# Graph attention and message passing on one core: relative node numbers spread over the partitions by TensorE in place of a DMA broadcast

## What is computed

```
# layer 0 (heads H = 4 of C = 32), per edge e = (src, dst):
alpha = sum(q[dst] * k[src], -1) / sqrt(C)
a     = softmax of alpha over the edges of one dst
conv  = segment_sum(a * v[src], dst) + x @ Wskip.T + bskip
#   then output projection, layer norm, a 512 wide MLP, layer norm
# layer 1, per edge: w = MLP(radial embedding of edge_weight)
#   messages = products of w, up(x)[src] and the direction edge_attr_3
out = segment_sum(messages, dst) @ W_out
```

## Time and profile before

| | |
|---|---|
| three runs | 2977.77, 2978.21, 2989.45 us, median 2978.21 |
| span of the profiled execution | 2979.6 us (what lies around it is not given apart) |
| busy, share of the span | PE 62%, PE weight loads 48%, DVE 56%, ACT 43%, POOL 53% |
| mean granted TensorE clock | 0.729 of full speed |
| DMA | 271.84 MB, mean 91 GB/s |

### The profile page before, as it was taken

One profiled execution on the slowest core, in us unless ns is written; L12 is line 12 of the kernel. 1 busy time (PEld: TensorE's weight loads), 2 busy tenths in 40 slices (PEclk: granted clock), 3 DMA queues, 4 the chain that ended last, 5 costly groups with the idle time before them and its releaser, 6 DMA issues. The chain is left out here.

```text
span 2979.6 us, 37370 instructions
## 1 busy us (share of the span) xinstructions
PE 1851.9 (62%) x9706; PEld 1441.9 (48%) x9706; DVE 1673.9 (56%) x4970; ACT 1271.8 (43%) x3058; POOL 1569.1 (53%) x1617
## 2 busy tenths in 40 slices
PE   3255454454554554454568177778787887887787
PEld 2244344354443444444555055555555555555556
DVE  2355555555554555554666055666656655666668
ACT  0245444455454555454545033434334334334345
POOL 4345455555555555555302756666666666666640
PEclk7556666656666666666678577888888778888889
DMA  6456454545555555544301211111111111111110
GB/s 213 135 140 170 134 136 133 138 135 144 142 137 137 140 143 138 145 130 134 109 2 35 53 39 43 45 47 44 45 45 44 45 44 44 44 44 46 46 36 24
DMA packets 242944, 271.84 MB, mean 91 GB/s; under 512 B 46236, under 2 KB 201970, under 8 KB 242220
## 3 DMA queue, kind: packets, MB, share of 16 engines
q0 software_dynamic: 64480, 158.57, 19.7%
q1 hardware_dynamic: 178252, 110.87, 13.6%
HBM read 257.11 MB, written 12.15 MB: 90 GB/s over the span
## 5 line engine op out<-in xcount | busy, mean ns | idle before, releaser
L476 POOL DMA_INDIRECT rows<-kv_tab,src_col x806 | 766.9, 951 | 691.5 <-DVE msg L1048 438.6
L490 POOL DMA_INDIRECT rows<-up_tab,src_col x806 | 796.4, 988 | 488.4 <-DVE rows L1362 240.9
L706 PE MATMUL ps<-hotT,rows 128*128 128x128 f32 x3232 | 511.1, 324 | 314.5 <-DVE rows L1369 164.5
L706 PEld LDWEIGHTS ps<-hotT,rows 128*128 128x128 f32 x3232 | 486.6, 235 | 365.4 <-DVE rows L1369 191.0
L524 PE MATMUL ps<-qwin,hotT 128*128 128x128 f32 x1616 | 357.4, 384 | 404.9 <-issue 194.5
L1333 DVE TENSOR_TENSOR acc<-acc,ps 128x256 f32 x808 | 338.1, 418 | 352.3 <-remote 207.1
L524 PEld LDWEIGHTS ps<-qwin,hotT 128*128 128x128 f32 x1616 | 320.1, 289 | 432.0 <-issue 335.7
L1065 DVE TENSOR_TENSOR acc<-acc,ps 128x128 f32 x808 | 228.0, 282 | 421.8 <-remote 329.4
L533 PE MATMUL ps<-hots,msg 128*128 128x128 f32 x1616 | 334.2, 373 | 48.9 <-DVE msg L1048 28.8
L533 PEld LDWEIGHTS ps<-hots,msg 128*128 128x128 f32 x1616 | 294.5, 273 | 81.3 <-DVE msg L1048 49.3
L757 ACT ACTIVATE hotT<-rel,consts 128x512 f32<-128x512 bf16 x202 | 145.0, 718 | 418.0 <-DMA qwin<-q_tab 303.6
(11 more groups left out here) (169 smaller groups left out, 2192.2 us busy)
## 6 DMA issues: line engine op xcount, KB each, us to landing
qwin<-q_tab SPq DMA_DIRECT2D x808, 64.0 KB
rel<-rel_far SPq DMA_DIRECT2D x202, 128.0 KB
rows<-kv_tab,src_col POOLq DMA_INDIRECT x806
rows<-up_tab,src_col POOLq DMA_INDIRECT x806
rows<-emb_rows SPq DMA_DIRECT2D x202, 16.0 KB
weights<-r_far SPq DMA_DIRECT2D x25, 128.0 KB
emb_rows<-weights SPq DMA_DIRECT2D x25, 128.0 KB
kv_tab<-rows SPq DMA_DIRECT2D x12, 256.0 KB, 2.8
```

The costliest lines, as they stand in the source:

```text
L476: nc.gpsimd.indirect_dma_start(kvr[:, q % RING, k, :], None, kv_tab, bass.IndirectOffsetOnAxis(src_col[:, t:t + 1].bitcast(U32), 0)).then_ ...
L490: nc.gpsimd.indirect_dma_start(upr[:, q % RING, k, :], None, up_tab, bass.IndirectOffsetOnAxis(src_col[:, t:t + 1].bitcast(U32), 0)).then_ ...
L706: mm = pe.matmul(ps[:, 4 + 2 * (q % 2) + k // 2, (2 * (k % 2) + m) * P:(2 * (k % 2) + m + 1) * P], left[:, q % 2, k, :], hot2[:, q % 2, k, ...
```

## The change

The relative numbers are no longer stored to DRAM. dst_rows and first_rows are laid out with two groups to a partition (101 partitions of 1024), DVE writes their difference as bfloat16 into an SBUF tile rel of the same shape, and an identity matrix in bfloat16 is kept. A new step of PE, spread(q), multiplies a column of that identity, broadcast over 128 columns, with the half row of rel, so that the 512 numbers of the group stand on all partitions of bank 7. ACT's Square reads them there. spread(q+3) stands in PE's slot q behind queries(q+1), the first two ahead of the loop. Bank 7 is shared with skip(i).

```diff
+        rel = sb("rel", [P, 2 * QC], BF16)
+        identb = sb("identb", [P, P], BF16)
+        dst_rows, first_rows = [yvec[0:NQ // 2, k * 2 * QC:(k + 1) * 2 * QC].bitcast(I32) for k in range(2)]
...
-            sp.wait_ge(rel_ready, 2)
-            sp.dma_start(rel_far.rearrange("(p n) -> p n", p=P), rel_rows).then_inc(rel_out, 16)
             sp.wait_ge(q_out, 16 * len(fours))
-            sp.wait_ge(rel_out, 16)
...
             def windows(q):
-                sp.dma_start(rel[:, q % RELS, :], rel_far[q * QC:(q + 1) * QC].partition_broadcast(P)).then_inc(q_in[q % 4], 16)
...
                 if q == 3:
                     batch_rows(0)
+                    sp.wait_ge(rel_ready, 2)
                     sp.dma_start(yvec[:], a["attr_col"]).then_inc(ld["attr"], 16)
...
+            def spread(q):
+                if q == 0:
+                    pe.wait_ge(rel_ready, 2)
+                    pe.wait_ge(identb_ready, 1)
+                else:
+                    pe.wait_ge(squareT_ready, q)
+                if q - 4 in SKIPS:
+                    pe.wait_ge(skip_sb, SKIPS.index(q - 4) + 1)
+                pe.matmul(ps[:, 7, :], identb[0:NQ // 2, q // 2:q // 2 + 1].to_broadcast([NQ // 2, P]),
+                          rel[0:NQ // 2, (q % 2) * QC:(q % 2 + 1) * QC], start=True, stop=True).then_inc(rel_mm, 1)
...
             def queries(q):
-                pe.wait_ge(q_in[q % 4], 16 * (QT + 1) * (q // 4 + 1))
+                pe.wait_ge(q_in[q % 4], 16 * QT * (q // 4 + 1))
...
             def skip(i):
-                if i:
-                    pe.wait_ge(skip_sb, i)
+                pe.wait_ge(squareT_ready, SKIPS[i] + 4)
...
+            for q in range(2):
+                spread(q)
             for q in range(-1, LAST_SLOT):
                 if q + 1 < NQ:
                     queries(q + 1)
+                if q + 3 < NQ:
+                    spread(q + 3)
...
             def turned(q):
-                act.wait_ge(q_in[q % 4], 16 * (QT + 1) * (q // 4 + 1))
                 if q >= TURNS:
                     act.wait_ge(qe_ready, q - TURNS + 1)
-                nc.scalar.activation(to, rel[:, q % RELS, :], ACT.Square, bias=consts[:, K_NEGP:K_NEGP + 1]).then_inc(squareT_ready, 1)
+                act.wait_ge(rel_mm, q + 1)
+                nc.scalar.activation(to, ps[:, 7, :], ACT.Square, bias=consts[:, K_NEGP:K_NEGP + 1]).then_inc(squareT_ready, 1)
...
-            v.tensor_tensor(rel_rows, dst_rows, first_rows, ALU.subtract).then_inc(rel_ready, 1)
+            v.tensor_tensor(rel[0:NQ // 2, :], dst_rows, first_rows, ALU.subtract).then_inc(rel_ready, 1)
             dve.wait_ge(ld["const"], 16)
+            v.tensor_copy(identb[:], ident).then_inc(identb_ready, 1)
...
-"dst_rows": (P, NT), "first_rows": (P, NT)
+"dst_rows": (NQ // 2, 2 * QC), "first_rows": (NQ // 2, 2 * QC)
```

More of the change, by code:

```diff
@@ L39 @@
 TURNS = 3
-RELS = 4
 CHAIN = 4
@@ L160, in build @@
         emb_rows = dram("emb_rows", [NB, NT * P])
-        rel_far = dram("rel_far", [NT * P], BF16)
         consts = sb("consts", [P, K_N])
@@ L177, in build @@
         hotT = sb("hotT", [P, TURNS, QT, P])
-        rel = sb("rel", [P, RELS, QC], BF16)
+        rel = sb("rel", [P, 2 * QC], BF16)
+        identb = sb("identb", [P, P], BF16)
         work = sb("work", [P, 2, QC])
@@ L232, in build @@
         hotf = rowsf[:, RING * QC:RING * QC + 16 * QC]
-        dst_rows, first_rows = [yvec[:, k * NT:(k + 1) * NT].bitcast(I32) for k in range(2)]
-        rel_rows = yvec[:, 2 * NT:2 * NT + NT // 2].bitcast(BF16)
+        dst_rows, first_rows = [yvec[0:NQ // 2, k * 2 * QC:(k + 1) * 2 * QC].bitcast(I32) for k in range(2)]
         kvr = rowsf.rearrange("p (s t f) -> p s t f", s=RING, t=QT)
@@ L277, in build @@
             sem("rel_ready"), sem("r_ready"), sem("r_out"), sem("emb_sq"), sem("emb_ready"), sem("pad_ready"))
-        rel_out, res_ready, row_sum = sem("rel_out"), sem("res_ready"), sem("row_sum")
+        rel_mm, identb_ready, res_ready, row_sum = sem("rel_mm"), sem("identb_ready"), sem("res_ready"), sem("row_sum")
         yprep, bprep, b2_in, const_ready, rows_ready = sem("yprep"), sem("bprep"), sem("b2_in"), sem("const_ready"), sem("rows_ready")
@@ L1408 @@
     "consts": (P, K_N), "vecs": (P, V_N), "weights": (P, W_N), "wqkv": (P, 3 * D), "bqkv": (3 * D,), "xT": (P, NW),
-    "src_col": (P, NT), "dst_col": (P, NT), "dst_first": (NT,), "dst_rows": (P, NT), "first_rows": (P, NT), "dst_lanes": (BATCHES * P, P + 2),
+    "src_col": (P, NT), "dst_col": (P, NT), "dst_first": (NT,), "dst_rows": (NQ // 2, 2 * QC), "first_rows": (NQ // 2, 2 * QC), "dst_lanes": (BATCHES * P, P + 2),
     "tile_ends": (BATCHES, 4 * H * HS), "r_col": (P, NT), "attr_col": (P, 3 * NT), "mlp_b2": (1, D),
@@ L1475, in layout @@
     a["dst_first"] = tiles[:, 0]
-    a["dst_rows"] = tiles.reshape(P, NT)
-    a["first_rows"] = np.repeat(tiles[:, 0], P).reshape(P, NT)
+    a["dst_rows"] = tiles.reshape(NQ // 2, 2 * QC)
+    a["first_rows"] = np.repeat(tiles[:, 0], P).reshape(NQ // 2, 2 * QC)
     around = np.empty((BATCHES, H, BT, P + 2), np.int32)
```

## The result

The changed kernel takes **3007.33 us** (five runs, 3002.74 to 3019.20), the kernel before 2984.41 (five runs, two of them new). The ratio is **1.0084**, interval 1.0062 to 1.0106: slower by some 25 us. The forecast was 41 us less, the range held the time, the sign was wrong. The profiled execution took 3008.59 us, its span is 3006.8.

A forecast was written before the change was run, and what follows sets the result against it. SP's pace and PE's late increments were taken to hold back each first-pass group. Terms +22 - 78 + 10 + 5 = -41 gave 2938.6 us for the profiled execution, 2937 for the median; eight-in-ten range 2850 to 3015.

The forecast's parts named there:

- The start: First loads: 101 partitions go through one DMA engine, delaying q_tab's stores and POOL; +22 us, ends -2 and +40.
- near 67: Sign at the start: the two loads land, and DVE's subtraction that uses them stands, near 67 us, before at 31.56.
- rival D: First loads: they spread over all 16 DMA engines; 2913 us for the kernel, chance 0.09.
- The rel load off SP: SP's queue, first pass: one of 14 instructions per group goes, at the fast price 0.42 x 186; -78 us, ends 0 and -150.
- rival C: First pass: window waits are hidden anyway, as DVE's wait for sums covers ACT's and PE's; 2990 us, chance 0.20.
- The window wanted later: ACT's turned(q) no longer waits for a window, only PE's queries(q) does; counted with SP's saved load, no us of its own.
- PE's product: PE, each group: a product of 512 bfloat16 columns, a tenth of 102 us on the path; +10 us, ends 0 and +102.
- The hand-over: Bank 7 has one buffer, passed between PE and ACT; costs only at seven skip slots, +5 us, ends 0 and +13.
- Rival B: PE's spread ahead of sums: bank 7's PE, ACT, PE round adds 3.2 x 35 = 112 us; 3049 us, chance 0.16.
- wrong if ACT waits for PE more than it waited for windows: Sign in the first pass against the forecast: ACT's wait for PE's product was to stay below its 227 us for windows.
- part 2: Removing the rel load from SP's queue in the first pass, forecast at -78 us.
- SP's wait for qe_ready: Sign for the windows: SP's wait for window slots, 29 us before, was to grow past 100 us.

The follow-up runs named there:

- experiment 2: Kernel before, without SP's rel load from the fifth group on and with turned(q) no longer waiting for the windows of its group; ratio 0.9924.
- the version that beats the kernel before: Changed kernel with loads of 112 partitions and spread(q + 3) at the end of PE's slot; 2972.24 us, ratio 0.9961 to the kernel before.

## Why the prediction was wrong, point by point

**1. The start: right in kind, a little large.** +22 was taken and 22 measured (1.0084 less 1.0010), but not of the same thing. The +22 was 24 and 3, less 5 for the rel loads that SP saves before the first weighing. The 22 is the price of 101 partitions against 112, both without those loads, so it stands against 27. Against the kernel before, the first weighing came 12.3 us later. L978 came at 65.26 for "near 67", the stores were done at 70 for 72, the 64th gather started at 129 for an end near 131. With 101 partitions the DMA share was 0.07, one engine, and with 112 it was 1.01. By the rule of the Trainium skill (DMA: Bandwidth & Descriptors, on why a DMA increments its semaphore by 16) a prime 101 gives one engine and 112 = 16 x 7 gives 16: the trace agrees. That pair excludes rival D.

**2. The rel load off SP: the step that failed.** -78 was taken, the fast price of 0.42 us times 186, on the ground that SP is the pace in the fast stretches; measured -18. The direction holds and the price per group is 0.09 us. The error was to carry the saved step of SP over to the end in full: of the time that was freed, 100 us came back as waits of SP itself. SP works 1111 of 1290 us, but in the pauses DVE has a chain of its own that ends as late. The pause of the earlier trace rows shows it; more rows of the kernel before, of the same time:

```profile
580.92 1.88 SPq L380 DMA_DIRECT2D qwin<-q_tab  x4
...
581.12 0.72 ACT L757 ACTIVATE hotT<-rel,consts 128x512 f32<-128x512 bf16 x1 [10.28 <-DMA qwin<-q_tab]
...
582.49 0.68 DVE L1048 TENSOR_TENSOR msg<-rows,ps 128x512 f32<-128x512 f32 x1
```

PE's late increment lets DVE go at 580.27. From there DVE works without a gap to the weighing at 582.49, and this weighing releases POOL's gather at 583.44. SP's rel load, its windows and ACT's square lie beside that chain, so a faster SP step does not bring this gather earlier. The 61 pauses over 0.9 us from 330 to 1440 us are alike in that. Followed back from the weighing that ends a pause, DVE's last wait is 24 times at the sums (L1065), 37 times at a step of the softmax chain (L1134 for ACT 19 times, L1086 for PE 11, L1093 7) and never at the product that needs the windows (L1029). SP can reach these waits only by way of ACT and PE; how much of the 0.09 us is that, no run shows. The prediction had this as rival C, with "a little of the SP step", 20 us, and gave it 0.20. ACT's 227 us for windows were read as proof of SP's pace; experiment 2 shows that they stood beside a late increment of PE.

**3. The window wanted later: right to count it as nothing of its own** (0.9924 against 0.9939), but not for the reason given. It did not bring the saved time to the end either.

**4. PE's product: right in kind, a little small.** +10 was taken, a tenth of 102 us; 7, 14 and 15 were measured. A product took 517 ns in the changed kernel and its weight load 121, where the nearest row gave 410 and 97. Pauses are about 30% of a batch (15.7 of 55.7 us). Moving the product behind the sums gives back 19 us with the changed kernel and 15 with its loads mended (1.0010 to 0.9961).

**5. The hand-over: about right.** +5 was taken, some 7 was measured, within its error. Rival B had the right sign for the wrong reason: its 112 us for late rounds did not come. That PE and ACT wait for each other was put down as a sign of it ("wrong if ACT waits for PE more than it waited for windows"), and the sign came, 305 us over 227. But the version that beats the kernel before has that wait at 332 us. The sign was badly chosen: a wait of one engine for another tells nothing of the time where both also wait for late increments.

**The sum** by measured terms is +22 - 18 + 15 + 7 = +26 us, and +25 was measured. The terms are a chain of kernels (without the load, with the product, with the hand-over, with the start); each is good to some 5 us, so the agreement to 1 us is luck. With the 7 us of the product alone the sum would be 18. Forecast and result differ by 66 us, and 60 of them are part 2. SP's wait for qe_ready was to pass 100 us and is 62; its freed time went to the wait at L396. Groups of 6.5 us were forecast: 1290 us over the 182 squares of the stretch are 7.09 (6.94 before).

## What to carry to other kernels

When an engine looks like the pace because it is hardly ever idle, ask in its fast stretches who else ends at the same time; of the instruction taken off SP here, a fifth of its duration came back. What is put in its place may cost more if it stands ahead of what the slowest chain waits for: moved to the end of the slot it gave back 15 to 19 us. And lay out a load so that 16 divides its partitions, with rows of zeros if need be: that gave back 22 us, more than any other single edit here. Of the three only the last also counted at the second level.

## What the runs showed of the hardware

- **The same program runs at two levels, 2980 to 3015 us and near 2237 us.** The same files gave both, and so did chips of the same number. At the first level DVE and ACT wait up to 15 us for increments of PE while gathers are issued, and batches take 55.7 us; at the second there is no such wait from 160 to 1000 us, and they take 40.3. The part behind the last weighing is shorter too, 1142 us for 1452 in the changed kernel, and the mean granted clock of the whole execution is 0.86 for 0.74. The runs do not show why. A result in which such waits decide should be taken as that of one level.
- **SP's slow steps belong to the first level as well.** The window loads of the changed kernel in the first fill, while POOL issues a gather every 1.25 us, first at 3007 us and then at 2256 us:

```profile
71.64 22.46 SPq L374 DMA_DIRECT2D qwin<-q_tab  x16
```
```profile
71.84 9.53 SPq L374 DMA_DIRECT2D qwin<-q_tab  x16
```

  That is 1.40 us for each load with its two register instructions, and 0.60. So the slow step of SP beside gathers, which the prediction took from the rows, is one of the first level.
- **A load on few DMA engines also holds its queue's issuer:** the second load of 101 partitions took 5.10 us to issue (0.43 with 112), and the seven stores behind it 36.84 (7.93). At the second level it was 5.85 and 36.86.
- **A small load was no cheaper to the kernel than a large one:** with 64 bytes in place of the 128 KB written by the broadcast, the issue took 0.31 us for 0.42 in the median, and the time stayed where it was (1.0004).
